# Graph attention: the second head's source-score row in PSUM banks of its own, its maxima ahead of the pairs, and an early small exponential

## What is computed

```python
h = (x @ W).reshape(N, heads, out_ch)
a_src = jnp.einsum('nhc,hc->nh', h, att_src)
a_dst = jnp.einsum('nhc,hc->nh', h, att_dst)
e = jax.nn.leaky_relu(a_src[src] + a_dst[dst], NEG_SLOPE)
m = jax.ops.segment_max(e, dst, num_segments=N)
ex = jnp.exp(e - m[dst])
s = jax.ops.segment_sum(ex, dst, num_segments=N)
alpha = ex / (s[dst] + 1e-16)
out = jax.ops.segment_sum(h[src] * alpha[:, :, None], dst, num_segments=N)
```

## Time and profile before

| | |
|---|---|
| median of 3 runs | 1345.88 us (1343.27 to 1350.83) |
| the profiled execution | 1350.56 us, span 1348.7 us |
| a1: the prologue, then its pairs | about 703 to 734 us, then to 924 us |
| a2: the prologue, then its pairs | about 924 to 972 us, then to 1177 us |
| busy share of the span | PE 80%, DVE 57%, POOL 46%, ACT 38% |
| mean granted TensorE clock | 0.879 of full speed |

### The profile page before, as it was taken

One profiled execution on the slowest core, in us unless ns is written; L12 is line 12 of the kernel. 1 busy time (PEld: TensorE's weight loads), 2 busy tenths in 40 slices (PEclk: granted clock), 3 DMA queues, 4 the chain that ended last, 5 costly groups with the idle time before them and its releaser, 6 DMA issues. The chain is left out here.

```text
span 1348.7 us, 17476 instructions
## 1 busy us (share of the span) xinstructions
PE 1080.3 (80%) x5532; PEld 748.1 (55%) x5536; DVE 774.1 (57%) x1693; ACT 518.9 (38%) x728; POOL 624.2 (46%) x501
## 2 busy tenths in 40 slices
PE   3999379979499999993985998788988887615696
PEld 1444267778477777771553887673644433114572
DVE  6888485437333333333956999851686876475133
ACT  2233443232111111110333688882376777731010
POOL 1000464302567555544114789891477777501543
PEclk9999699965699999996896999998989999955796
DMA  3000000325489999954100111202011111008454
GB/s 106 0 1 0 1 1 2 124 85 190 144 294 293 304 302 308 299 175 151 47 5 29 39 55 35 64 16 65 32 47 33 38 42 41 15 0 297 153 198 142
DMA packets 110379, 140.62 MB, mean 104 GB/s; under 512 B 30900, under 2 KB 74516, under 8 KB 110312
## 3 DMA queue, kind: packets, MB, share of 16 engines
q1 hardware_dynamic: 93832, 114.54, 26.0%
q0 software_dynamic: 16480, 25.24, 5.6%
HBM read 138.71 MB, written 29.81 MB: 125 GB/s over the span
## 5 line engine op out<-in xcount | busy, mean ns | idle before, releaser
L1650 POOL TENSOR_TENSOR am<-CT,qb 128x1024 f32<-128x1024 f32 x128 | 299.3, 2366 | 66.5 <-ACT PT L1670 32.6
L1761 DVE TENSOR_TENSOR am<-PS,am 128x1024 f32<-128x1024 f32 x128 | 156.5, 1223 | 55.9 <-ACT PS L1663 41.0
L1755 DVE CUSTOM_DVE_ANT_0 masked<-PS,mask 128x1024 f32<-128x1024 f32 x128 | 156.1, 1219 | 39.4 <-issue 35.4
L1663 ACT ACTIVATE PS<-adb,ab 128x1024 f32<-128x1024 f32 x128 | 143.1, 1118 | 85.9 <-DVE am L1761 85.8
L1197 DVE COPY yo<-PS 128x512 f32<-128x512 f32 x79 | 54.6, 692 | 207.1 <-PE PS L1135 207.1
L1882 PE MATMUL PS<-h,PT 128*128 128x129 f32 x1024 | 129.8, 285 | 39.3 <-ACT PT L1670 25.8
L1127 PE MATMUL PS<-xgT,w1r 128*128 128x128 f32 x1264 | 156.9, 278 | 0.0
L1895 PE MATMUL PS<-PT,h 128*65 128x512 f32 x256 | 127.8, 637 | 33.4 <-ACT PT L1670 17.1
L1162 ACT ACTIVATE hT<-PS,b1T 128x128 f32<-128x128 f32 x158 | 49.5, 364 | 266.8 <-PE PS L1127 266.8
L1127 PEld LDWEIGHTS PS<-xgT,w1r 128*128 128x128 f32 x1264 | 150.2, 195 | 1.5 <-issue 1.5
L1882 PEld LDWEIGHTS PS<-h,PT 128*128 128x128 f32 x1024 | 122.9, 198 | 49.3 <-issue 37.2
(11 more groups left out here) (326 smaller groups left out, 1590.3 us busy)
## 6 DMA issues: line engine op xcount, KB each, us to landing
w2r<-in_L_ffn_W SPq DMA_DIRECT2D x79, 512.0 KB, 6.7
w1r<-in_L_ffn_W SPq DMA_DIRECT2D x79, 512.0 KB, 4.7
adb<-a_scratch SPq DMA_DIRECT2D x16, 512.0 KB, 3.7
qb<-q_scratch SPq DMA_DIRECT2D x14, 512.0 KB, 3.7
wc<-in_L_gnn_W SPq DMA_DIRECT2D x4, 1024.0 KB, 8.1
x_res<-in_x SPq DMA_DIRECT2D x1, 2048.0 KB, 10.3
W2t<-in_L_gnn_W SPq DMA_DIRECT2D x2, 1024.0 KB
out<-x_res SPq DMA_DIRECT2D x8, 256.0 KB, 3.4
```

The source lines that it names most:

```text
L1650: pool.tensor_tensor(am[:, k % RING, :], CT[:, s, :], qb[:, hd % 2, :], ALU.add).then_inc(s_sum, 1)
L1663: act.activation(RELU, adb[:, hd % 2, :], ACT.Relu, bias=ab[:, s, hd:hd + 1]).then_inc(s_relu, 1)
L1755: dve.tensor_tensor_reduce(masked[:], ASB, mask[:, t, :], 1.0, -3.0e38, ALU.subtract, ALU.max, mrow[:, hd % 2, t:t + 1]).then_inc(s_max, 1)
L1761: dve.tensor_tensor(am[:, k % RING, :], RELU, am[:, k % RING, :], ALU.add).then_inc(s_all, 1)
```

## The change

For both layers:

- `a_row(1)` writes to banks of its own: 1 and 2 in a1, 2 and 3 in a2 (`row_bank`). PE issues it straight behind the first unit of `h`, without a wait for head 0's maxima. `maxed(1, t)` reads these banks.
- All eight maxima of head 1 stand ahead of the pairs on DVE. `FIRST` then has 9 maxima for the pairs of head 0, where it had 12. PE waits for all sixteen before its first pair.
- `a_row(2)` comes ahead of pair 0's gather on PE, where it was ahead of pair 1's. q(1) comes behind POOL's pair 1 (was 4), q(2) behind its pair 10 (was 7).
- `q_row` writes to the ReLU banks 4 and 5, so relu(0) waits for the copy to `qb`.
- ACT issues an exponential of 128x1 behind the three `a3` copies of the prologue.
- In a1 three units of `h` stand ahead of the pairs (were two), in the banks 0, 3, 0. The third is multiplied behind q_row(0) and copied behind relu(0), and PE waits for that copy ahead of its first pair. The other three come at the pairs (0, 1), (0, 5) and (1, 1); (2, 1) has none any more.

```diff
+        warm = place("warm", [P, 1], F32, 97 * KIB + 928)
...
-            RELU, ASB = wide(4), wide(6)
+            RELU = wide(4)
+            SECOND = 2 if final else 1
+
+            def row_bank(hd):
+                return SECOND if hd == 1 else 6
+
+            def unit_bank(i):
+                return i % 2 if final else (0, 3, 0)[i]
...
-                H0 = 2
-                H_AT = (0, 1), (0, 5), (1, 1), (2, 1)
+                H0 = 3
+                H_AT = (0, 1), (0, 5), (1, 1)
...
-            EARLY = 5
-            FIRST = {0: ((1, 5),), 1: ((1, 6),), 2: ((1, 7),), 3: ((2, 0), (2, 1)), 4: ((2, 2), (2, 3)),
-                     5: ((2, 4), (2, 5)), 6: ((2, 6), (2, 7)), 7: ((3, 0),)}
+            FIRST = {**{s: ((2, s),) for s in range(5)}, 5: ((2, 5), (2, 6)), 6: ((2, 7),), 7: ((3, 0),)}
...
-            A_ROW = {1: 2, **{8 * (hd - 3) + 6: hd for hd in range(3, HEADS)}}
-            Q_AFTER = {4: 1, 7: 2, **{NT * (hd - 1) + 2: hd for hd in range(3, HEADS)}}
+            A_ROW = {0: 2, **{8 * (hd - 3) + 6: hd for hd in range(3, HEADS)}}
+            Q_AFTER = {1: 1, **{NT * (hd - 1) + 2: hd for hd in range(2, HEADS)}}
...
                     act.copy(a3[64:64 + 2 * HEADS, :], rest[:]).then_inc(s_a3, 1)
+
+                    act.activation(warm[:], ident[:, 0:1], ACT.Exp)
...
                     act.wait_ge(s_q0, 1)
-                    act.copy(qb[:, 0, :], PS[:, 2:4, :].rearrange("p a n -> p (a n)")).then_inc(s_q0m, 1)
+                    act.copy(qb[:, 0, :], RELU).then_inc(s_q0m, 1)
                     if not final:
                         act.wait_ge(s_bias, 16)
                     act.wait_ge(s_bm, 2)
+                    act.wait_ge(s_q0m, 1)
                     relu(0)
...
-                    for t in range(NT):
-                        maxed(0, t)
-                    for t in range(EARLY):
-                        maxed(1, t)
+                    for hd in range(2):
+                        for t in range(NT):
+                            maxed(hd, t)
...
-                        wait(pe, s_max, NT * hd)
+                        wait(pe, s_max, NT * (hd if hd > 2 else hd - 1))
...
-                            mm = pe.matmul(PS[:, 2 + t // 4, (t % 4) * P:(t % 4 + 1) * P],
+                            mm = pe.matmul(PS[:, 4 + t // 4, (t % 4) * P:(t % 4 + 1) * P],
...
-                        h_tile(i, i % 2)
-                        if i == (H0 - 3 if final else H0 - 1):
+                        h_tile(i, unit_bank(i))
+                        if i == 0:
+                            pe.wait_ge(s_bm, 1)
+                            a_row(1)
+                        if i == (H0 - 3 if final else 1):
                             q_row(0)
-                            a_row(1)
                     if final:
                         pe.wait_ge(s_w[1], 16)
                     pe.wait_ge(s_hm, H0)
-                    pe.wait_ge(s_q0m, 1)
                     pe.wait_ge(s_ones, 1)
+                    pe.wait_ge(s_max, 2 * NT)
```

More of the change, by code:

```diff
@@ L1697, in _ @@
                     act.copy(a3[0:2 * HEADS, :], aTs[:]).then_inc(s_high, 1)
-                    h_moved(0, 0)
+                    h_moved(0, unit_bank(0))
                     act.wait_ge(s_rest, 1)
                     act.copy(mid[:], rest[:]).then_inc(s_mid, 1)
-                    h_moved(1, 1)
+                    h_moved(1, unit_bank(1))
                     act.wait_ge(s_mid, 1)
@@ L1705, in _ @@
                     act.copy(a3[64:64 + 2 * HEADS, :], rest[:]).then_inc(s_a3, 1)
+                    act.activation(warm[:], ident[:, 0:1], ACT.Exp)
                     for i in range(2, H0 - 2):
-                        h_moved(i, i % 2)
+                        h_moved(i, unit_bank(i))
                     act.wait_ge(s_q0, 1)
-                    act.copy(qb[:, 0, :], PS[:, 2:4, :].rearrange("p a n -> p (a n)")).then_inc(s_q0m, 1)
+                    act.copy(qb[:, 0, :], RELU).then_inc(s_q0m, 1)
                     if not final:
@@ L1754, in maxed @@
                         dve.memset(spare[:, t:t + 1], 0.0)
-                        dve.tensor_tensor_reduce(masked[:], ASB, mask[:, t, :], 1.0, -3.0e38, ALU.subtract, ALU.max,
+                        dve.tensor_tensor_reduce(masked[:], wide(row_bank(hd)), mask[:, t, :], 1.0, -3.0e38, ALU.subtract, ALU.max,
                                                  mrow[:, hd % 2, t:t + 1]).then_inc(s_max, 1)
@@ L1854, in a_row @@
                             for half in range(2):
-                                mm = pe.matmul(PS[:, 6 + half, :], sel[0:A3, hd:hd + 1].to_broadcast([A3, P]),
+                                mm = pe.matmul(PS[:, row_bank(hd) + half, :], sel[0:A3, hd:hd + 1].to_broadcast([A3, P]),
                                                a3[0:A3, half * 512:(half + 1) * 512], start=True, stop=True)
@@ L1859, in a_row @@
                         for half in range(2):
-                            mm = pe.matmul(PS[:, 6 + half, :], ident[0:2 * HEADS, hd:hd + 1].to_broadcast([2 * HEADS, P]),
+                            mm = pe.matmul(PS[:, row_bank(hd) + half, :], ident[0:2 * HEADS, hd:hd + 1].to_broadcast([2 * HEADS, P]),
                                            aTs[:, half * 512:(half + 1) * 512], start=True, stop=True)
```

## The result

The changed kernel takes 1332.99 us (median of 11 runs, 1332.17 to 1340.55) beside 1345.88 for the kernel before (11 runs, 1341.49 to 1350.83). The ratio is 0.9914, with a 95% interval of 0.9897 to 0.9931: 9.3 to 13.9 us less. Forecast were 10.7 us less, 1335.2.

A forecast was written before the change was run, and what follows sets the result against it. DVE was taken to set a1's pace, idle behind late work on PE's queue. Gains of 7.5 us in a1 and 3.2 in a2 made 10.7, from the median 1345.88 to 1335.2 us; 8-in-10 range 1330.5 to 1342.

The forecast's parts named there:

- The maxima of a1: a1's start: all sixteen maxima run without a gap, first pair added at 729.1 instead of 734.28; nominally 9.0 us on DVE.
- The third unit and the clock: a1 before maximum (2, 0): h_tile(2) partly at PE's half clock leaves DVE idle 0.9 us, bounds 0 and 2.3.
- What is next late: a1, head 0: PE's queue delays maximum (3, 0), idle 1.5 us; pair 8 at 753.9 against 761.35, a1 gains 7.5.
- The exponential: a1's prologue: the table load moves into ACT's idle time near 720, giving back 1.1 us before the third pair's addition.
- q(1) and q(2): a1, POOL's rows: the later q(2) costs nothing, with 2.4 us to spare on a 16.0 us DMA trip.
- rival (C): Head 2's row: q(2)'s DMA trip grows past 18.4 us and delays pair 16; 1349 at 32 us; chance 0.04.
- a2: Second attention layer: pair 1's columns 1.1 us sooner, head 1's first columns 2.3 sooner; gains 3.2 us, bounds 0 and 3.4.
- The further 1.1 us: a2, head 1's first two columns: shorter PE idle time before them makes them faster by up to 1.1 us.
- The sum: Whole kernel: 7.5 + 3.2 = 10.7 us less than the median 1345.88, so 1335.2 us.
- main case: Whole kernel: the summed gains hold, giving 1333 to 1338 us; chance 0.58.
- rival (B): Clock returns early in a1, a2 keeps 3.4: 11.9 us, or 13 to 14 if PE waits shrink: 1332; chance 0.15.

The follow-up runs named there:

- row_behind_q: Changed kernel, but PE issues a_row(1) behind q_row(0) again in both layers; ratio 1.0044 to the kernel before, 5.9 us slower.
- no_small_exp: Changed kernel without the small exponential in the prologue; ratio 0.9923 to the kernel before.
- a2_only: Kernel before with the change in the second attention layer alone; ratio 0.9978, 3.0 us less.
- both: Changed kernel with a1's units at (0, 1), (0, 6), (2, 1), first copied a pair later, and matmuls filling a2's head changes; 1327.27 us, ratio 0.9897.
- a1_only: Kernel before with the change in the first attention layer alone; ratio 0.9942, 7.8 us less.
- before_again: The kernel before, profiled once more unchanged; a2 took 239.5 us from its start to its last pair.
- hold_clock: Changed kernel with seven extra fp32 matmuls on PE at each head change of a2; ratio 0.9903 to the kernel before.

## Why the prediction was right, and where it was not

**The maxima of a1**: as forecast. Pair 0 is added 20.35 us after the first maximum (forecast 20.4, before 25.6). row_behind_q shows that it is the place of a_row(1) on PE's queue.

**The third unit and the clock**: the term was mis-sized. I took 0.9 us of idle time before maximum (2, 0), with q_row at the half clock throughout. PE's idle time before it was 2.85 us, since a_row(1) and unit 1 now stand in it; q_row took 2.50 us instead of the 3.79 of the earlier trace rows, unit 2 was through at 726.8, before the sixteenth maximum, and a_row(2) waited only for the maxima. No idle time at (2, 0).

**What is next late**: PE, as forecast, but not by the steps that I gave. The sum for DVE alone (751.1) counts one maximum too many, 1.27 us: between the additions of pair 1 and pair 7 and maximum (3, 0) there are seven maxima, (2, 1) to (2, 7), and not eight. Rightly counted the wait before (3, 0) would have been 2.7 us and not 1.5; measured were 2.23 there and 1.68 before pair 5, which I overlooked and where ACT's copy of unit (0, 1) holds the ReLU. None of this moves the forecast of pair 8, since that goes by PE's queue. There I had taken 1.82 us for each gather, and the first two took 5.28 us together; the granted clock was 0.50 of full speed in their first 2 us and 0.74 in the next. Pair 1 was added 1.0 us sooner than forecast, and of that PE lost 0.7 again: pair 8 came 44.96 us after the first maximum (forecast 45.2). That pair 8 came so close is luck: a wait at (2, 0) that wasn't there, against gathers slower than I had taken them.

**The exponential**: the load stands at 719.32 (forecast near 720), in ACT's idle time, with the small exponential 1.30 us behind its start. The Trainium skill ("ScalarE: Activation LUTs", What ACT_TABLE_LOAD costs) puts a drain of about 1.38 us behind a load. It shows in no row here, in this place or in no_small_exp's, where the exponential starts 1.30 us after the load began, and by these rows a load costs its 1.28 us. The 1.1 us before pair 2 are there (no_small_exp); they were mis-sized for what comes of them, 2.4 us at pair 8 and in the like profile at pair 16, and in the time of the whole kernel nothing of it can be told.

**q(1) and q(2)**: right that they cost nothing, the room was nearer 6 us than 2.4. I had taken the longest trip, 16.0 us; this one was some 15. What I said against rival (C), that the same trip costs DVE nothing at the later heads, is wrong by the trace of before itself: at the first pair of head 6 DVE waits 2.75 us for POOL, which had waited for that row.

```profile
869.67 6.99 POOL L1650 TENSOR_TENSOR am<-CT,qb 128x1024 f32<-128x1024 f32 x3 [3.46 <-DMA qb<-q_scratch]
...
872.05 1.23 DVE L1761 TENSOR_TENSOR am<-PS,am 128x1024 f32<-128x1024 f32 x1 [2.75 <-POOL am L1650]
```

At head 7 it is 3.49 us. The profile of the changed kernel has 2.54 and 3.33 there, that of the changed kernel again only 1.73 at head 7 and none for POOL at head 6. From pair 24 to the last pair of a1 it is 106.9 us in the first profile of either kernel and 103.7 and 103.4 in the second. This belongs to neither kernel, and it is a place where a1 still loses time.

**a2**: 3.0 us alone (0.9 to 5.1) for 3.2 forecast. The first maximum isn't a good mark to count from, since the copy of the last early unit comes 24.8 to 27.5 us behind it in either order. Counted from that copy, which the forecast rightly took as fixed by PE, the first exponential comes 1.3 us later in the new order (before 1.4), pair 1's columns 5.84 us later (before 6.97, so 1.1 sooner, as forecast), and head 1's first columns 27.5 us later in seven profiles (28.1 in a2_only and both). The order of before has 30.2, 29.4 and, in a1_only, 30.7. Between profiles with the same time from the maximum to the copy that is 1.8 us sooner (changed, before_again) and 2.55 (a2_only, a1_only), forecast 2.3. The copy, pair 1's columns and head 1's first columns of the changed kernel, beside the earlier trace rows:

```profile
961.57 0.37 ACT L1697 COPY h<-PS 128x256 f32<-128x256 f32 x1 [3.08 <-PE PS L1878]
...
967.41 1.90 PE L1906 MATMUL PS<-PT,h 128*65 128x512 f32 x4 [1.34 <-ACT PT L1678]
...
989.10 1.93 PE L1906 MATMUL PS<-PT,h 128*65 128x512 f32 x4 [2.15 <-ACT a_oT L1685]
```

The further 1.1 us that I expected from the shorter idle time before them is a matter of chance: from the first column to the unit behind the second it took 3.92 us in this profile and 5.18 in another with the same 2.15 us of idle time.

**The sum**: 10.7 us, measured 9.3 to 13.9 and again 8.5 to 14.0. The measured ratio is 11.6 us, which lies between the main case and rival (B): there was no wait at (2, 0), as (B) had it, but the time that this gave wasn't kept up to pair 8. The profiled pair differs by 17.2, and a reader who had only those two traces would have credited a2 with 6 us that are the clock's.

## What to carry to other kernels

An operand that is ready but stands late on its engine's queue costs what its consumer waits: give it a place and a buffer of its own where the queue has slack, and move the consumer's work up only together with it. row_behind_q did the second without the first and lost 5.9 us against before. When such a wait goes, list every operation that the freed engine meets next, with the engine that issues it; here one wait was missed and another mis-sized, and only PE's queue, which ended last, gave the right sum, in part by luck. And compare stages over several profiles before a gain is put down to a change.

## What the hardware showed that I had not expected

PE's granted clock after one and the same idle stretch differs from execution to execution: after 2.41 us of idle time in a2 two columns took 3.93 us in one profile of the changed kernel and 5.18 in another, at several head changes of each. In the first it held at all of them, in the second it fell at the first five; other profiles are mixed (before_again holds it at two of five). a1 does the same with two gathers after 2.38 us, 3.81 or 5.45 us. Behind 1.8 us or less no profile here shows a fall at a head change. With 1.72 us of matmuls put into the stretch, which left 0.6 to 0.9 us idle, the clock stayed full in both kernels that had them.

The head changes of a2 are worth 2.4 us of its stage and not more (pair 8 to the last pair: 168.0 us with the full clock, 170.4 with the half). hold_clock, which has the full clock at each of them, still takes 239.8 us for the stage, since its start to the first maximum was a slow one (21.16 us). With what differs at its start and up to pair 8, the stage takes 236.6 or 241.9 us for the same instructions: nearly half of what the change is worth in all.
